# Layernorm of a graph transformer: the two feature halves of each chunk are added on GpSimd before TensorE sums over the partitions

## What is computed

```python
def _layernorm(x, axis=-1, eps=1e-05):
    m = jnp.mean(x, axis=axis, keepdims=True)
    v = jnp.var(x, axis=axis, keepdims=True)
    return (x - m) / jnp.sqrt(v + eps)
...
    xn = _layernorm(x, axis=-1)
    x = x + gnn(xn, ...) + mix(xn[None], ...)[0]
    x = x + ffn(_layernorm(x, axis=-1)[None], ...)[0]
```

## Time and profile before

| what | value |
|---|---|
| median of three timed executions | 7826.95 us (7817.87 to 7835.87) |
| the profiled execution: its own time | 7832.94 us |
| its span in the trace | 7830.9 us |
| granted TensorE clock over the span, share of full speed | 0.81 |
| busy shares: TensorE, VectorE, ScalarE, GpSimd | 74%, 52%, 35%, 39% |
| the first parts of the nine layernorms together | 225.75 us |

### The profile page before, as it was taken

One profiled execution on the slowest core, in us unless ns is written; L12 is line 12 of the kernel. 1 busy time (PEld: TensorE's weight loads), 2 busy tenths in 40 slices (PEclk: granted clock), 3 DMA queues, 4 the chain that ended last, 5 costly groups with the idle time before them and its releaser, 6 DMA issues. The chain is left out here.

```text
span 7830.9 us, 89819 instructions
## 1 busy us (share of the span) xinstructions
PE 5814.7 (74%) x21954; PEld 3665.6 (47%) x21954; DVE 4058.4 (52%) x9875; ACT 2727.9 (35%) x7590; POOL 3063.3 (39%) x3135
## 2 busy tenths in 40 slices
PE   5564677777984788866966777897788848997476
PEld 3332454543542555542534553454565535665243
DVE  7875456662112899955245334214466675556401
ACT  2533366651220344410104432111555515554010
POOL 1775444522771666610007750000455505553001
PEclk9999677677997788878988888898777666887588
DMA  2534211110001655500013330000333313333122
GB/s 90 153 104 129 52 32 37 38 19 26 2 2 43 167 158 160 159 20 13 0 47 106 105 72 2 23 1 20 97 89 94 91 41 110 91 100 73 57 103 71
DMA packets 268803, 547.54 MB, mean 70 GB/s; under 512 B 86992, under 2 KB 136589, under 8 KB 263949
## 3 DMA queue, kind: packets, MB, share of 16 engines
q0 software_dynamic: 134496, 314.63, 16.1%
q1 hardware_dynamic: 133932, 228.62, 9.1%
HBM read 493.99 MB, written 49.00 MB: 69 GB/s over the span
## 5 line engine op out<-in xcount | busy, mean ns | idle before, releaser
L1459 POOL DMA_INDIRECT L3a_edges_rows<-scratch_L3a,L3a_edges_index x416 | 404.9, 973 | 922.2 <-DMA L3a_edges_last<-order_dst_last 544.9
L1459 POOL DMA_INDIRECT L_edges_rows<-scratch_L_kv,L_edges_index x416 | 511.2, 1229 | 436.1 <-PE L_edges_ps_sum L1704 194.1
L628 POOL DMA_INDIRECT L_edges_rows<-scratch_L,L_edges_index x416 | 393.6, 946 | 609.9 <-SPq L612 483.5
L1459 POOL DMA_INDIRECT L_edges_rows<-scratch_L,L_edges_index x416 | 409.4, 984 | 537.8 <-DVE L_edges_msg L1506 290.0
L1459 POOL DMA_INDIRECT L3b_edges_rows<-scratch_L3b,L3b_edges_index x416 | 398.9, 959 | 413.6 <-PE L3b_edges_ps_sum L1704 246.1
L482 POOL DMA_INDIRECT scratch_by_dst<-dst_record,dst_dest x400 | 442.5, 1106 | 271.6 <-DVE dst_dest L334 150.0
L2481 DVE TENSOR_TENSOR L_experts_gated_h<-L_experts_hidden,L_experts_ps_g 128x800 f32<-128x800 f32 x112 | 110.6, 987 | 694.1 <-PE L_experts_ps_g L2434 694.1
L1580 DVE TENSOR_TENSOR L_acc<-L_edges_ps_sum,L_acc 128x264 f32 (+1 forms) x832 | 357.2, 429 | 155.6 <-PE L_edges_ps_sum L1704 86.0
L482 POOL DMA_INDIRECT scratch_by_src<-src_record,src_dest x400 | 383.1, 958 | 139.1 <-issue 121.7
L2472 ACT ACTIVATE L_experts_hidden<-L_experts_ps_h,L_eb_sb 128x400 f32<-128x400 f32 x320 | 189.8, 593 | 665.3 <-PE L_experts_ps_h L2427 665.3
L1704 PE MATMUL L3a_edges_ps_sum<-L3a_edges_rows,L3a_edges_hot 128*128 128x264 f32 x832 | 378.3, 616 | 1.3 <-DVE L_acc L1580 1.2
(11 more groups left out here) (771 smaller groups left out, 13195.9 us busy)
## 6 DMA issues: line engine op xcount, KB each, us to landing
x<-scratch_dst_key_rows SPq DMA_DIRECT2D x50, 512.0 KB, 4.9
x<-scratch_src_key_rows SPq DMA_DIRECT2D x50, 512.0 KB
L_experts_w<-in_L_w SPq DMA_DIRECT2D x16, 1024.0 KB
L_edges_rows<-scratch_L,L_edges_index POOLq DMA_INDIRECT x832, 2.8
L_edges_lo_rows<-order_src_lo_rows SPq DMA_DIRECT2D x52, 256.0 KB
L3a_edges_lo_rows<-order_dst_lo_rows SPq DMA_DIRECT2D x52, 256.0 KB
L3b_edges_lo_rows<-order_dst_lo_rows SPq DMA_DIRECT2D x52, 256.0 KB
x<-scratch_dst_lo_rows SPq DMA_DIRECT2D x50, 256.0 KB, 3.7
```

Of the source, the lines that this page charges most:

```text
L628: pool.indirect_dma_start(rows[:, n % RING, k, :], None, row_table, bass.IndirectOffsetOnAxis(index[:, t:t + 1].bitcast(U32), 0)).then_inc ...
L1459: pool.indirect_dma_start(rows[:, n % RING, k, 0:RW], None, row_table, bass.IndirectOffsetOnAxis(index[:, t:t + 1].bitcast(U32), 0)).then_ ...
```

## The change

GpSimd gets code in the stage. For each chunk it adds the two feature halves of `src` into `half` (one of three buffers), and the two halves of `square` into `fold` (one of two). Each is a two-input float32 add with a result of 128x400. TensorE then runs one matmul for the mean on `half` and one for the variance on `fold`, in place of two each. `mean(c)` waits for `halved`, `variance(c)` waits for `folded`, and ScalarE waits for `folded` where it waited for `spread`. The second part of the stage is the same.

```diff
+        half = s.sb("half", [P, 3, CW])
+        fold = s.sb("fold", [P, 2, CW])
...
                 def mean(c):
                     if c >= 3:
                         pe.wait_ge(centred, c - 2)
-                    for f in range(2):
-                        ins = nc.tensor.matmul(ps_mean[:, c % 3, 0:CW], kit.mean[:], chunk(src, c)[:, f], start=f == 0,
-                                               stop=f == 1)
-                    ins.then_inc(averaged, 1)
+                    pe.wait_ge(halved, c + 1)
+                    nc.tensor.matmul(ps_mean[:, c % 3, 0:CW], kit.mean[:], half[:, c % 3, :], start=True, stop=True
+                                     ).then_inc(averaged, 1)

                 def variance(c):
-                    pe.wait_ge(squared, c + 1)
-                    for f in range(2):
-                        ins = nc.tensor.matmul(ps_var[0:NC, 0:CW], kit.mean_to[:, c, :], square[:, c % 2, f, :],
-                                               start=c == 0 and f == 0, stop=c == NC - 1 and f == 1)
-                    ins.then_inc(spread, 1)
+                    pe.wait_ge(folded, c + 1)
+                    nc.tensor.matmul(ps_var[0:NC, 0:CW], kit.mean_to[:, c, :], fold[:, c % 2, :], start=c == 0,
+                                     stop=c == NC - 1).then_inc(spread, 1)
...
+            @block.gpsimd
+            def _(pool):
+
+                def add_halves(c):
+                    if c >= 3:
+                        pool.wait_ge(averaged, c - 2)
+                    nc.gpsimd.tensor_tensor(half[:, c % 3, :], chunk(src, c)[:, 0], chunk(src, c)[:, 1],
+                                            ALU.add).then_inc(halved, 1)
+
+                for c in range(3):
+                    add_halves(c)
+                for c in range(NC):
+                    pool.wait_ge(squared, c + 1)
+                    if c >= 2:
+                        pool.wait_ge(spread, c - 1)
+                    nc.gpsimd.tensor_tensor(fold[:, c % 2, :], square[:, c % 2, 0], square[:, c % 2, 1],
+                                            ALU.add).then_inc(folded, 1)
+                    if c + 3 < NC:
+                        add_halves(c + 3)
+
             @block.scalar
...
                     if c >= 2:
-                        act.wait_ge(spread, c - 1)
+                        act.wait_ge(folded, c - 1)
```

More of the change, by code:

```diff
@@ L1848, in layernorm @@
             s.sem(n) for n in ("averaged", "centred", "squared", "spread", "rooted", "inverted", "sent", "normed", "chain"))
+        halved, folded = s.sem("halved"), s.sem("folded")
         def chunk(y, c):
```

## The result

The median of five timed executions is 7787.12 us (7781.32 to 7794.43), against 7826.95 before. The ratio is 0.9948, 95% interval 0.9935 to 0.9961: faster by 31 to 51 us. In a later comparison on one chip the same kernel had 7776.35 us against 7832.52, ratio 0.9928 (0.9912 to 0.9944). The forecast was 7774, its range 7753 to 7808.

The account below looks back on a forecast made before the run. TensorE's instruction stream was taken to bound the nine layernorm first parts; with GpSimd adds of 0.95 us each norm would take 19.1 in place of 25.0 us, saving 53 in all: 7827 − 53 = 7774 us, range 7753 to 7808.

Parts of the forecast that it names:

- TensorE was the bound, and its loss of records is worth what the records cost: First part of each norm: TensorE's turn falls from 2.98 to 1.64 us with four records in place of eight.
- GpSimd becomes the bound with two adds a turn: Turn of each norm's first part: GpSimd has 1.90 us, above TensorE's 1.64 and VectorE's 0.99.
- The add takes 0.95 us: Each GpSimd add of 400 columns: 0.95 us taken, with bounds of 0.52 and 1.20.
- Two whole copies: Alternative size for one GpSimd add, as two one-input copies with their fixed parts: 1.04 us.
- the estimate with the fixed part of the copies in it: GpSimd add of 400 columns, in proportion from the skill page's 4497 ns with 0.18 us fixed: 1.03 us.
- The sum of one norm: First part of one norm, on TensorE's old start: 19.1 us in place of 25.0, 5.9 saved.
- The start: GpSimd 0.26 us later than TensorE: After the barrier before each norm: GpSimd starts 1.17 us after the last VectorE instruction, TensorE 0.91.
- The code fetch and the two semaphores, costed at nothing: GpSimd's code fetch and the two new semaphores: no cost added to the forecast.
- The gaps before the first and the last fold: GpSimd in each norm's first part: idle before fold0 only, and more briefly before fold7.
- Rival, exclusion of GpSimd's reads and VectorE's subtract: First parts: eight subtracts of 0.99 us join GpSimd's chain, 27.0 us a norm, 18 us slower in all; chance 0.06.
- Rival, an add far dearer than three passes: GpSimd adds: gain gone from 1.44 us an add, 17 us slower in all at 1.6; chance 0.05.
- Rival, the clock stays at 1.2 GHz: TensorE, less busy, keeps a 2.98 us turn; 5 us slower in all, 7832, no difference; chance 0.04.

Follow-up runs that it names:

- experiment 1: Changed kernel, but GpSimd adds only the halves of src and the variance is summed by two matmuls again: 7794.29 us, ratio 0.9961 to the kernel before.
- experiment 2: Changed kernel, but GpSimd adds only the halves of the squares and the mean is summed by two matmuls of src: 7795.83 us, ratio 0.9965.
- experiment 5: Changed kernel with GpSimd adding 200 of each chunk's 400 columns, the rest constants, matmuls kept: ratio 0.9916 to the kernel before, on a slower chip.
- experiment 6: Changed kernel with each GpSimd add twice as wide (128x800), TensorE reading the half with the sum: ratio 1.0016 to the kernel before, on a slower chip.
- experiment 3: Changed kernel with the adds of the squares' halves moved to VectorE, those of src staying on GpSimd: 7762.74 us, ratio 0.9924 to the kernel before.
- experiment 7: The best version: experiment 3 with each mean one chunk earlier in TensorE's order; ratio 0.9902 to the kernel before, later 7743.86 us on a faster chip.
- experiment 8: Experiment 4 with each mean one chunk earlier in TensorE's order: ratio 0.9904 to the kernel before, on a slower chip.
- experiment 4: Changed kernel with four half buffers in place of three, so four adds of src precede the first fold: 7776.95 us, ratio 0.9942 to the kernel before.

## Why the prediction was right, point by point

- *TensorE was the bound, and its loss of records is worth what the records cost.* Right, shown by experiments 1 and 2 (2.31 us with six records) and 5 (1.64 with four).
- *GpSimd becomes the bound with two adds a turn.* Right, shown by the timeline after and by experiments 5 and 6: with longer adds the first part grows by 12.3 times what one add gains, with shorter ones it stops at TensorE's turn.
- *The add takes 0.95 us.* This term was mis-sized: 1.035 in the mean. Adds that follow one another start 0.99 apart, so the turn is 1.98 us and not 1.90. The rows gave the fixed 0.18 us well (0.61 us at 200 columns and 1.035 at 400 leave 0.18 at none), but the second input costs more than a second pass of a copy: 2.14 ns an element against 2 × 0.85. Two whole copies, 1.04, would have met the size, but by luck: they hold the fixed part twice and would give 0.70 us at 200 columns, where 0.61 was measured. The Trainium skill's "GPSIMD Engine Reference", section "Performance versus the Vector engine", gives about 2.6 cycles an element and 4497 ns for 2,048. Worked out again, the estimate with the fixed part of the copies in it is 1.02 us, not the 1.03 of the prediction; the trace has 1.035, and agrees.
- *The sum of one norm.* It has 18.86 us from GpSimd's first add on (19.12 less the 0.26 of the start); measured are 19.8 in eight norms and 19.0 in the one with gamma. Of the 0.9 us by which it was short, 0.2 lie between the first add and the first fold, where the first mean and its way out took 1.74 us at 1.2 GHz and not 1.53; 0.5 in ten adds at 0.05 more each; 0.2 in the last chunk, its longer fold and its handovers. Nine norms: 8 us.
- *The start: GpSimd 0.26 us later than TensorE.* Wrong: 0.22 in the second norm alone, 0.03 on average over the nine. The rows set GpSimd behind one kind of stage (1.17 us) against TensorE behind another (0.91); behind the same stage the two differ by 0.02 in most norms. This error gives back 2 us of the 8, so that part of the closeness is luck: about 48 us saved in the first parts where 53 were forecast. The code fetch and the two semaphores, costed at nothing, cost nothing that shows.
- *The gaps before the first and the last fold*: right, 1.80 and 0.96 us.
- *Rival, exclusion of GpSimd's reads and VectorE's subtract.* Did not come. With a subtract beside it an add takes 1.04 us in the median and at most 1.08, without one 1.03; the subtract, which always has an add beside it now, takes 0.99 as before. The exclusion is real for a VectorE add whose two inputs both lie in SBUF (experiment 3). This is how the page "SBUF — State Buffer", section "Who interferes with whom", of the Trainium skill divides the cases, and here both sides of its rule are measured.
- *Rival, an add far dearer than three passes.* Did not come; experiment 6 shows what it would have done: at 1.70 us an add the kernel is slower than before.
- *Rival, the clock stays at 1.2 GHz.* Did not come: in the changed kernel no pair in mid-part stands at 1.2 GHz. With the double-width adds of experiment 6, where TensorE idles for about half of each turn of 3.3 us, most turns are still at 2.4 GHz, but in the third, fourth and ninth norm a few are not. One variance pair of the third norm takes 1.50 us in place of 0.84:

```profile
3268.34 1.50 PE L1870 MATMUL L_norm_ps_var<-L_norm_fold,mean_to 128*8 128x400 f32 x2
```

  It cost nothing there, since GpSimd sets the turn: all nine norms take 27.9 us.

## What to carry to other kernels

Cost a move of work between engines by the turn of every engine after the move, not by what the old bound loses: here TensorE could have gone from 2.98 to 1.64 us a turn, and GpSimd's two adds stopped it at 1.98. Then ask which third engine has room: VectorE was busy for 7.9 of 19.8 us, and with one of the two adds there the turn came down to 1.64. When a gap on the bound engine closes and the time hardly moves, look for the same gap further on in another engine's queue: here the fourth buffer alone gave 0.3 us a norm, and with TensorE's order changed as well 2.0. The new order with three buffers was not run.

## What the runs showed of the hardware

- A two-input float32 add on GpSimd, both inputs and the result in SBUF: 0.61 us for 128x200, 1.035 for 128x400. For 128x800 with one input repeated it is 1.70 us, less than the 1.89 that the first two lengths give; whether the repeated input or the longer shape makes it cheaper was not tried.
- GpSimd's add and VectorE's two-input add on SBUF hold each other up, in both directions (VectorE 0.57 to 1.44 us; GpSimd 1.03 to 1.45 in the best version). A fold that started beside an add ended 0.43 us after it, both with 1.01 and with 0.17 us of the add left. VectorE's subtract with one input in PSUM does not.
- Weight loads and waits: a change between two matmul groups costs TensorE about 0.15 us in each version whose turn TensorE sets (turns of 2.98, 2.31 and 1.64 us), so four records a turn cost 1.64 and not 1.33 us. Which part of it is the semaphore and which the weight load stays open.
- One chip took about 1,090 us longer than another for the kernel before, 376 of them ahead of the first norm (traces of experiments 8 and 4), where TensorE was as busy on both. The norms' first parts did not change: the version of experiment 7 has 146.4 us on the one and 146.3 on the other. What made the rest slower was not tried.
- The first instruction of a stage came 0.60 to 0.95 us after the last VectorE instruction on TensorE and 0.62 to 1.17 on GpSimd, by the kind of the stage before (seven norms each; ahead of the other two something else is waited for).
